# An attention stage: output gates spread by DMA, the softmax divisor multiplied once, and a value block in another place

## The reference

```python
gv = _gate(x, Wsel_v)          # sigmoid scores of 8 experts a head, the two largest kept
v = einsum('bsd,bhse,hedp->bhsp', x, gv, Wv)
att = softmax(einsum('bhsp,bhtp->bhst', q, k) / sqrt(P))      # 16 heads, P = 64
o = einsum('bhst,bhtp->bhsp', att, v)
go = _gate(x, Wsel_o)
return einsum('bhsp,bhse,hepd->bsd', o, go, Wo)
```

## Time and profile before

| | |
|---|---|
| median of three runs | 4017.39 us (4015.6 to 4018.32) |
| profiled execution, its own time | 4015.01 us |
| its span, first to last instruction | 4013.1 us, TensorE's clock 0.98 of full speed on the mean |
| busy over the span | PE 3720.9 (93%), DVE 3230.8 (81%), POOL 2739.0 (68%), ACT 2025.4 (50%) |
| DMA | 131.91 MB, 33 GB/s on the mean |

### The profile page before, as it was taken

One profiled execution on the slowest core, in us unless ns is written; L12 is line 12 of the kernel. 1 busy time (PEld: TensorE's weight loads), 2 busy tenths in 40 slices (PEclk: granted clock), 3 DMA queues, 4 the chain that ended last, 5 costly groups with the idle time before them and its releaser, 6 DMA issues. The chain is left out here.

```text
span 4013.1 us, 55149 instructions
## 1 busy us (share of the span) xinstructions
PE 3720.9 (93%) x16064; PEld 2547.5 (63%) x16064; DVE 3230.8 (81%) x3744; ACT 2025.4 (50%) x3758; POOL 2739.0 (68%) x2876
## 2 busy tenths in 40 slices
PE   6999999998669999999999999999999999999786
PEld 2444444444357777777777777777777777777675
DVE  4998899999558787878787878787777878787698
ACT  5666676666334454444454545454445454445343
POOL 3777788787556676676677667667667667766354
PEclk9999999999889999999999999999999999999898
DMA  2110111111030010000001001001001000000011
GB/s 76 53 43 32 64 68 69 37 37 58 32 131 16 10 45 10 16 29 25 10 16 39 16 16 39 10 10 44 16 10 44 11 16 16 11 16 11 34 42 37
DMA packets 53665, 131.91 MB, mean 33 GB/s; under 512 B 4222, under 2 KB 33790, under 8 KB 47072
## 3 DMA queue, kind: packets, MB, share of 16 engines
q1 hardware_dynamic: 52560, 127.02, 8.8%
q0 software_dynamic: 1040, 4.19, 0.3%
HBM read 114.16 MB, written 17.04 MB: 33 GB/s over the span
## 5 line engine op out<-in xcount | busy, mean ns | idle before, releaser
L383 POOL TENSOR_TENSOR state<-state,c_rows 128x1024 f32<-128x1024 f32 x256 | 604.1, 2363 | 219.9 <-DVE state L838 218.9
L1336 ACT ACTIVATE prob<-ps_b,negmax 128x512 f32<-128x512 f32 x512 | 345.9, 686 | 660.1 <-DVE negmax L1455 660.1
L838 DVE TENSOR_TENSOR_SCAN state<-dA,ps_a 128x1024 f32<-128x1024 f32 x256 | 585.0, 2285 | 48.1 <-PE ps_a L521 21.7
L1449 DVE TENSOR_TENSOR vg<-ps_b,gates 128x1024 f32<-128x1024 f32 x256 | 313.4, 1224 | 252.3 <-PE ps_b L1174 237.6
L1063 POOL TENSOR_TENSOR qk_full<-vg 128x512 f32<-128x512 f32 x256 | 329.2, 1286 | 253.2 <-DVE vg L1449 253.2
L707 ACT ACTIVATE dA<-dt,a_neg 128x511 f32<-128x511 f32 x512 | 338.6, 712 | 311.0 <-DVE state L838 310.5
L521 PE MATMUL ps_a<-state,ident 128*128 128x512 f32 x1024 | 482.8, 594 | 0.4 <-POOL state L383 0.4
L1076 POOL TENSOR_TENSOR ogT_low<-prob,ogT_high 128x512 fp32r<-128x512 f32 x256 | 324.1, 1301 | 209.1 <-ACT ogT_high L1369 209.1
L1172 PE MATMUL ps_b<-ogT_high,wo_high 128*128 128x512 f32 x1024 | 413.3, 404 | 11.1 <-DVE ogT_low L1501 10.8
L1172 PE MATMUL ps_b<-wv_high,xT_high 128*128 128x512 f32 x1024 | 415.0, 405 | 9.0 <-DVE vg L1449 6.7
L1174 PE MATMUL ps_b<-ogT_high,wo_low 128*128 128x512 f32 x1024 | 404.9, 395 | 0.0
(11 more groups left out here) (239 smaller groups left out, 8683.0 us busy)
## 6 DMA issues: line engine op xcount, KB each, us to landing
xT<-xT_scratch SPq DMA_DIRECT2D x65, 512.0 KB, 3.3
c_rows<-c_scratch SPq DMA_DIRECT2D x32, 1024.0 KB, 5.0
wv<-in_wv SPq DMA_DIRECT2D x8, 1024.0 KB, 4.9
wo<-in_wo SPq DMA_DIRECT2D x8, 1024.0 KB, 7.0
x_in<-in_x SPq DMA_DIRECT2D x8, 512.0 KB, 4.8
x_a<-in_x SPq DMA_DIRECT2D x8, 512.0 KB, 6.7
x_scratch<-x_a SPq DMA_DIRECT2D x8, 512.0 KB, 2.8
xT_scratch<-x2T SPq DMA_DIRECT2D x8, 512.0 KB, 2.7
```

Of the source, the lines that this page charges most:

```text
L383: pool.tensor_tensor(state, state, c_rows[:, n, :].unsqueeze(1).to_broadcast([P, HALF, S]), ALU.mult).then_inc(hc_done, 1)
L838: dve.tensor_tensor_scan(h[s % RING][:, :, :].rearrange("p c s -> p (c s)"), dA[s % RING][:, :, :].rearrange("p c s -> p (c s)"), ps[:, DB ...
L1336: act.activation(prob[h][:, t, :], ps[:, score_bank(t) + h, :], ACT.Exp, bias=negmax[:, t, h:h + 1], accum_out=total[:, h, t:t + 1]).then_ ...
```

## The change

The gates are turned as they are, early in the iteration, copied to `gT`, stored to a scratch tensor in HBM and loaded back with each expert's row repeated over 64 partitions. `wide[0]`, for the first four experts of each head, lies in the buffer of the low parts `ogT[1]`, `wide[1]` in a new one. The reciprocal divisor is copied along 64 columns for each head, turned by four transposes, and multiplied into the output once (`scale_parts`), in PSUM. `gate_outputs` multiplies that by the wide gates. The spread table, its matmuls, and high and low parts of the gates are gone. TensorE's first value block of the next iteration goes ahead of `project`, but for a pair's last iteration, behind which `pair_start` has it. On VectorE, the fourth gated pair now follows `turn_raw` and the first low output, and the third low output goes ahead of `rotate`.

```diff
@@ SP
+            def widen(it):
+                sp.wait_ge(gT_done, it + 1)
+                sp.wait_ge(wide_loaded, CREDIT + it * 64)
+                sp.sem_inc(held, 1)
+                sp.dma_start(d["gates"].rearrange("h e s -> (h e) s"), gT[:, :]).then_inc(gT_stored, 16)
+                sp.wait_ge(gT_stored, CREDIT + it * 16 + 16)
+                sp.wait_ge(out_psum, CREDIT + it * KD)
+                sp.sem_inc(held, 1)
+                for half in range(2):
+                    for h in range(2):
+                        rows = d["gates"][h, half * EP:(half + 1) * EP, :].rearrange("e s -> (e s)").partition_broadcast(HP)
+                        sp.dma_start(wide[half][h * HP:(h + 1) * HP].rearrange("p e s -> p (e s)"), rows).then_inc(wide_loaded, 16)
...
                     load_xT(b + 1)
+                    widen(j * NB + b)
+                sp.wait_ge(xT_low, CREDIT + j * NB + NB)
+                load_xT(0)
                 if more:
                     sp.wait_ge(gates_done, j * NB + NB)
                     load_scores(j + 1)
-                sp.wait_ge(xT_low, CREDIT + j * NB + NB)
-                load_xT(0)
+                widen(j * NB + (NB - 1))
...
-            sp.dma_start(vg[:, 0:2, :, :].rearrange("p t e n -> p (t e n)"), d["spread"]).then_inc(consts_loaded, 16)
@@ TensorE
             def turn_gates(it):
-                pe.wait_ge(gate_step, CREDIT + it * GATE + GATE)
+                pe.wait_ge(gates_done, it + 1)
+                pe.wait_ge(acc_done, CREDIT + it)
                 for t in range(TT):
-                    mm = pe.transpose(ps[:, GT_BANK, t * P:(t + 1) * P], out_gate[:, t, :], ident[:, :])
+                    mm = pe.transpose(ps[0:2 * E, GT_BANK, t * P:(t + 1) * P], gates[:, t, 2 * E:4 * E], ident[:, :])
                 mm.then_inc(gT_psum, 1)
+            def turn_shares(it):
+                pe.wait_ge(share_done, it + 1)
+                for t in range(TT):
+                    mm = pe.transpose(ps[:, SHARE_BANK, t * P:(t + 1) * P], share_wide[:, t, :], ident[:, :])
+                mm.then_inc(share_psum, 1)
...
             def batch(it, j, b, more, more_pairs):
-                pe.wait_ge(w_low["wv"], j * 2 + 2)
-                values(it, 0, 0)
                 values(it, 0, 1)
                 scores(it, 0)
                 scores(it, 1)
+                turn_gates(it)
...
-                turn_gates(it)
                 for c in range(TT):
                     attend(it, 1, c)
-                spread_gates(it, 0)
-                spread_gates(it, 1)
+                turn_shares(it)
                 if more or more_pairs:
...
                     project_raw(it + 1, 0)
-                spread_gates(it, 2)
-                if more or more_pairs:
                     project_raw(it + 1, 1)
-                spread_gates(it, 3)
+                if more:
+                    pe.wait_ge(oT_done, it * 2 + 1)
+                    values(it + 1, 0, 0)
                 for n in range(N):
                     project(it, j, n)
@@ ScalarE: copy_gates(it) is the first of batch, high_gates(it) is gone
+            def copy_gates(it):
                 act.wait_ge(gT_psum, it + 1)
+                act.wait_ge(gT_stored, CREDIT + it * 16)
+                act.activation(gT[:, :], ps[0:2 * E, GT_BANK, :], ACT.Copy).then_inc(gT_done, 1)
@@ VectorE
-            def output_gates(it):
+            def shares(it):
                 dve.wait_ge(exp_done, it * 2 * TT + 2 * TT)
-                dve.reciprocal(share[:, :, :], total[:, :, :]).then_inc(gate_step, 1)
...
+                dve.reciprocal(share[:, :, :], total[:, :, :]).then_inc(share_step, 1)
+                dve.wait_ge(share_step, it + 1)
+                dve.tensor_copy(share_wide[:, :, :].rearrange("p t (h n) -> p t h n", h=2),
+                                share[:, :, :].rearrange("p h t -> p t h").unsqueeze(3).to_broadcast([P, TT, 2, HP])).then_inc(share_done, 1)
...
+            def scale_parts(it):
+                dve.wait_ge(oT_done, it * 2 + 2)
+                dve.wait_ge(share_psum, it + 1)
+                dve.tensor_tensor(ps[:, SCALED_BANK, :], oT[:, :], ps[:, SHARE_BANK, :], ALU.mult).then_inc(scaled, 1)
...
+                bank = GATED_BANK[e // 2]
+                dve.tensor_tensor(ps[:, bank:bank + 2, :] if half else og[:, e:e + 2, :], ps[:, SCALED_BANK, :].unsqueeze(1).to_broadcast([P, 2, S]),
+                                  wide[half][:, e:e + 2, :], ALU.mult).then_inc(og_done, 1)
...
-                low_gates(it)
                 add_parts(it, 1)
+                scale_parts(it)
                 gate_outputs(it, 0)
                 gate_outputs(it, 1)
                 if more or more_pairs:
                     tops(*coming, 1)
                 gate_outputs(it, 2)
-                gate_outputs(it, 3)
                 if more or more_pairs:
                     turn_raw(it + 1)
                 low_outputs(it, 0)
+                gate_outputs(it, 3, more or more_pairs)
+                low_outputs(it, 1)
                 if more or more_pairs:
                     swap_halves(it + 1)
-                low_outputs(it, 1)
+                low_outputs(it, 2)
                 if more:
                     tops(*coming, 2)
                 if more or more_pairs:
                     rotate(it + 1)
-                low_outputs(it, 2)
                 low_outputs(it, 3)
```

More of the change, by code:

```diff
@@ L986, in _ @@
         def _(sp):
-            for s in (v_psum, s_psum, out_psum, acc_done, vsum_done, og_done, xT_low, gate_step, top_done, rank_step):
+            for s in (v_psum, s_psum, out_psum, acc_done, vsum_done, scaled, wide_loaded, gT_stored, xT_low, top_done, rank_step):
                 sp.sem_inc(s, CREDIT)
@@ L1119, in rank_four @@
                 pool.wait_ge(rank_step, step + 3)
-                pool.wait_ge(gate_step, CREDIT + it * GATE)
+                if used is not None:
+                    pool.wait_ge(vg_done, used * 4 + 4)
+                    pool.wait_ge(gT_psum, used + 1)
                 pool.sem_inc(held, 1)
@@ L1161, in batch @@
                     rank_three(it + 1)
-                    rank_four(it + 1, ahead)
-            pool.memset(out_gate[:, :, :], 0.0).then_inc(zero_done, 1)
+                    rank_four(it + 1, ahead, it)
             low_x(0)
@@ L1190, in values @@
                     pe.wait_ge(vg_done, it * 4 + p - 1)
+                elif PAIR_BANK[p] + t % 2 == GT_BANK and p == 1:
+                    pe.wait_ge(gT_done, it + 1)
                 for c in range(KD):
@@ L1238, in attend @@
                 mm.then_inc(pv_psum, 1)
[L1240 to L1249, removed]
             def project(it, j, n):
@@ L1269, in start, with pair_start @@
                 project_raw(0, 1)
+            def pair_start(j):
+                pe.wait_ge(w_low["wv"], j * 2 + 2)
+                values(j * NB, 0, 0)
             def batch(it, j, b, more, more_pairs):
-                pe.wait_ge(w_low["wv"], j * 2 + 2)
-                values(it, 0, 0)
                 values(it, 0, 1)
@@ L1367, in high_outputs @@
                     act.wait_ge(e_psum, it * (N - 1) + n - EP + 1)
-                gated = ps[:, SPREAD_BANK[n // 2] + n % 2, :] if h else og[:, e, :]
+                gated = ps[:, GATED_BANK[e // 2] + n % 2, :] if h else og[:, e, :]
                 act.activation(ogT[0][:, e, :], gated, ACT.Copy).then_inc(oT_high, 1)
@@ L1410, in batch @@
                     high_qk(it + 1)
-            act.wait_ge(consts_loaded, 16)
-            act.activation(spread[:, :, :].rearrange("p b m -> p (b m)"), vg[:, 0:2, :, :].rearrange("p t e n -> p (t e n)"),
-                           ACT.Copy).then_inc(consts_done, 1)
             high_x(0)
@@ L1471, in low_probabilities @@
                                   ALU.subtract).then_inc(pT_low, 1)
-            def low_gates(it):
-                dve.wait_ge(gT_high, it + 1)
-                rows = slice(LOW_ROW, LOW_ROW + 2 * E)
-                low = gT[rows, :]
-                dve.tensor_tensor(low, ps[rows, GT_BANK, :], low.bitcast(F32), ALU.subtract).then_inc(gT_low, 1)
             def add_parts(it, h):
@@ L1535, in batch @@
                     low_probabilities(it, n)
-                output_gates(it)
+                shares(it)
                 if more or more_pairs:
@@ L1938, in layout @@
         out[name] = np.stack([table * np.float32(Q_SCALE), table], axis=1)
-    row = np.arange(E)[:, None] + np.arange(P)[None, :] // HP * E
-    takes = (np.arange(2 * E)[:, None, None] == row[None]).astype(np.float32).reshape(2 * E, BLOCKS * P)
-    spread = np.zeros((P, BLOCKS * P), np.float32)
-    spread[:2 * E] = spread[LOW_ROW:LOW_ROW + 2 * E] = takes
-    out["spread"] = spread
     out["w1"], out["w2"] = rows(f["W1"], KD), rows(f["W2"], FB)
@@ L1956, in program @@
     d["scores"] = nc.dram_tensor("scores_scratch", (PAIRS, P, NB, TT, GP), F32, kind="Internal").ap()
+    d["gates"] = nc.dram_tensor("gates_scratch", (2, E, S), F32, kind="Internal").ap()
```

59 lines of the change are left out of this document (24 added, 35 removed).

## The result

| | before | after |
|---|---|---|
| median of five runs | 4017.81 us (4015.6 to 4018.5) | 4041.77 us (4034.27 to 4044.11) |
| ratio to before | | 1.006, 95% interval 1.005 to 1.0071 |
| profiled execution, its time and its span | 4015.01, 4013.1 | 4038.08, 4036.3 |
| TensorE busy, mean clock | 3720.9 (93%), 0.98 | 3630.6 (90%), 0.97 |
| DMA | 131.91 MB | 267.73 MB |

The forecast was 4015.3 in 3999 to 4037; the time is 24 us above before. TensorE has 90 us less to do and the kernel takes longer, so the question is where TensorE now stands idle.

A forecast was written before the change was run, and what follows sets the result against it. The projection was taken to be bound equally by TensorE's order and a relay through the other engines. Terms -9.0 + 5.1 + 0.7 - 1.3 + 0.9 + 1.5 = -2.1 took 4017.4 to 4015.3 us, range 3999 to 4037.

The forecast's parts named there:

- Ordinary iteration, -0.16: From one projection's start to the next, the terms sum to -0.16 us, times 56 makes -9.0.
- The value block: Six matmuls moved from the iteration's head into TensorE's wait before the projection: -1.39 us.
- The relay: Chain from head 1's attend to the projection; multiplying the divisor in once on VectorE lengthens it by 0.73 us.
- The turned gates: Four transposes of raw gates at the iteration's head, after the second scores: +0.50 us, bounds 0.20 and 0.75.
- Pair boundaries, +0.73: At seven pair boundaries TensorE gives back the wait it saves, leaving the divisor multiplication's +0.73 us each: +5.1.
- Ends: First iteration +0.73 us, start -1.3, last iteration +0.92, and the clock falling earlier there +1.5, bounds 0 and 4.
- Step 9: Gate store and wide-gate loads on SP's queue: about 17 us after the projection's end, needed about 25 after, so hidden.
- A: Rival: wide gates land late at pair starts, by 0 to 2.6 us, eight times, up to +21, 4036; chance 0.12.
- E: Rival: clock falls in every iteration for the idle 0.6 and 1.1, 1.6 us each, 63 times, 4115; chance 0.03.
- B: Rival: POOL's gates come later than the turn on TensorE, 0.5 us lost 56 times, +28, 4043; chance 0.10.
- C: Rival: wide-share copy holds GpSimd's last value sum, up to 0.4 us each, 64 times, +26, 4041; chance 0.05.
- D: Rival: the turn between the heads did hold TensorE; without it -0.44 us x 56 = -25, 3990; chance 0.10.

The follow-up runs named there:

- block_back: w_later with the first value block put back at the head of the iteration; median 4107.35 us, ratio 1.0226.
- turn_twice: w_later with four more transposes of the raw gates, result unused, between the heads where the turn used to stand; median 3999.35 us, ratio 0.9967.
- low2_back: w_later with VectorE's third low output put back behind the rotation; median 4003.38 us, ratio 0.998.
- bcast128: Changed kernel, wide gates in two 1 MB loads to 128 partitions, head 0's gates for both heads; median 4005.51 us, ratio 0.998.
- w_later: Changed kernel with the next pair's weight loads issued behind the first xT and first wide gates; median 4001.24 us, ratio 0.9968.
- halves: Changed kernel, weights still ahead, with VectorE waiting for each half of the wide gates separately; median 4007.71 us, ratio 0.9991.
- fill18: Changed kernel, weights still ahead, with 18 useless matmuls on TensorE before the projection in every iteration; 4156.53 us in one run.

## Why the prediction was wrong

- **Ordinary iteration, -0.16:** measured -0.28, right in mechanism. The value block gave 1.37 of its 1.39 (block_back). The relay cost +0.81 instead of +0.73, for the wait behind the multiplication. The turned gates cost 0.36, not 0.50: the row they were taken from contained a pipeline's end that the next matmuls hide. The 0.08 that is left lies between the two heads' attends (4.57, before 4.65), and why isn't known; not for the turn, since turn_twice has 4.56.
- **Pair boundaries, +0.73:** +0.9 where no DMA is late. The give-back is right (low2_back).
- **Ends:** the last relay is 0.72 longer (of 0.92), but its interval is among the 56 ordinary ones and was shortened by 0.30: that term was counted twice. The clock behind it cost 0.35 (of 1.5). Ahead of the first projection -0.6 was forecast, and 2.7 more were measured; the scatter there hides what the start gained.
- **The step that failed is 9, "Hidden"**, with A, its rival. Step 9 reckoned an ordinary iteration, where it holds (landed 18.0 after the projection's end, used 24.9 after it; the step's own terms add up to 16, not to its 17), and left the boundary to A at 0.12. A's mechanism, place and threshold were right: "from 9.4 us after xT's landing"; the gates landed 12.1 after it, and VectorE waited 2.57. Two terms were mis-sized. The 2 MB took 11.9, not 5 to 10, for a rate read from loads to 128 partitions (bcast128). The store took 7.0, not 1.6, behind the weights, but the chain from xT's landing hides nearly all of that: the first load is issued 0.2 after it. Reckoned from xT's landing, then, the lateness is the loads' rate; w_later and halves show that it can be taken away in two other places as well. The waits came out about A's highest bound, 2.6 (2.4 to 3.1), seven times and not eight, for the last pair start has no weights to load.
- **What A left out** is the clock. It priced the wait and not what follows: 1.35 to 2.7 at each of seven late projections, 13.9 in all, which less the ordinary gain of 0.28 each is the +9.5 and +2.5 in the table above (fill18). E asked whether the gaps of 0.6 and 1.1 would lower the clock, rightly said no, and wasn't asked again for A's gap of 3.6. Against the forecast the boundaries are 16.8 worse, the other 56 intervals together 7.3 (9.5 and 2.5 less 13.7, for -9.0), the last iteration 2.0 better and the part ahead of the first projection 3.3 worse: 25.4, and the profiled execution is 25.2 above its forecast of 4012.9.
- **B:** the list of waits has VectorE behind POOL's gates. TensorE waits for them in the first iteration and at five boundaries, never in an ordinary iteration:

```profile
DVE vg L1463 <- POOL gates L1140: 48.7, 59, 2.6
```
```profile
2455.18 0.60 PE L1243 MATMUL ps_b<-ident,gates 128*16 128x128 f32 x4 [0.75 <-POOL gates L1140]
```

- **C:** the copy of the share takes 0.49 to 0.51 in ordinary iterations, where it begins beside GpSimd's last value sum, and 0.43 where it doesn't, as in the row below (the prediction's estimate was 0.3). The sum takes 0.46 as before, and head 1's attend comes no later (4.57 behind head 0's, before 4.65):

```profile
2470.17 0.43 DVE L1476 COPY share_wide<-share 128x512 f32<-128x512 f32 x1
```

- **D:** not borne out: the ordinary interval is 39.68 with the turn between the heads and without it (turn_twice).
- **The total of -2.1** is, with the queue mended and against its control, -4.6 by medians: of the forecast's sign, though a difference this small is hardly told from the scatter. The change was slower than before because its loads start behind the weights, run at 64 partitions' rate, and were all waited for at once; each of three repairs takes one of these away, and each suffices at the boundaries.

## What to carry to other kernels

A transfer that is hidden in the ordinary iteration has to be reckoned once more at the place where its queue is fullest, with the rate of its own shape and with what stands ahead of its store. A wait on the busiest engine is priced with the clock behind it: here gaps of 1.1 ahead of an ordinary projection cost only themselves, gaps of 1.7 to 2.5 in some passes 0.4 to 1.6 more and in others nothing, the seven late ones (2.5 to 4.1) each 1.35 to 2.7 more. And a clock loss counts only where TensorE is what others wait for: the projection ahead of a boundary loses 0.9 to 1.1 in five of seven passes of turn_twice, and the boundary stays at 44.35. A control that moves the same queue in the old kernel is worth its run: some 10 of the 40 us that the mended order gained were not the change's.

## What the runs showed that was not expected

- Loads to 64 partitions each, several in flight, move 224 GB/s together with the DMA engines fully busy; loads to 128 partitions move 369.
- Loads with two in their outermost dimension moved 53 GB/s at a DMA share of 0.13, and took the kernel from 4001 to 5693 us.
- Work without use made the kernel faster: four transposes in a wait of 1.7 us kept the clock up at every boundary, where it had fallen at three of seven for 0.4 to 0.8.
